# Three adapters around an attention and MLP block: laying x and the weights out feature-major and loading adapter 1's whole, on one core

## The reference

```python
def adapter(role, h0, W_down, b_down, W_up, b_up, gamma, beta):   # blocks 0, 2, 3
    h = gelu(h0 @ W_down[role] + b_down[role])                    # 256 -> 128
    y = h0 + h @ W_up[role] + b_up[role]                          # 128 -> 256
    return layernorm(y) * gamma[role] + beta[role]

def block1(x, target_codes):
    attn = softmax((x @ Wq) @ (x @ Wk).T / 16)                    # 32 x 32 for each sequence
    attn_out = attn @ (x @ Wv) @ Wp + bp
    cms_out = gelu(attn_out @ cW1 + cb1) @ cW2 + cb2 + one_hot(target_codes)
    modifier = gelu(concat(attn_out, cms_out) @ mW1 + mb1) @ mW2 + mb2
    return clip(x + cms_out + modifier, 0, 1)
```

## Time and profile before

| what | value |
|---|---|
| three runs | 195.41, 195.46, 195.92 us; median 195.46 |
| the profiled execution's own time | 195.86 us |
| its span, first to last instruction | 194.1 us |
| TensorE busy | 184.4 us, 95% of the span |
| VectorE busy | 114.2 us, 59% |
| ScalarE busy | 81.0 us, 42% |
| GpSimd busy | 42.2 us, 22% |
| DMA packets, bytes | 18,874 packets, 17.83 MB |

### The profile page before, as it was taken

The page is one execution under the profiler, slowest core; times in us unless marked ns, Lnnn a source line. Parts: engine busy times, 40 slices in busy tenths (PEclk is TensorE's granted clock), DMA queues, the critical chain, the costliest instruction groups (busy, mean ns, idle before and its releaser), DMA issues.

```text
span 194.1 us, 3155 instructions
## 1 busy us (share of the span) xinstructions
PE 184.4 (95%) x1031; PEld 158.1 (81%) x1031; DVE 114.2 (59%) x283; ACT 81.0 (42%) x164; POOL 42.2 (22%) x72
## 2 busy tenths in 40 slices
PE   7979999989999999999999999999999999999980
PEld 7858887979988888778888888888888989999860
DVE  2897998899658707983193532041432136558983
ACT  0643764544698306672055444003445323222340
POOL 8375657100000006000150000000100012226431
PEclk9999999999999999999999999999999999999997
DMA  3778579994301230330000061000100003441122
GB/s 105 233 206 285 156 254 286 261 295 159 108 3 17 93 108 0 108 111 0 0 0 3 0 181 35 0 0 5 54 0 0 3 0 106 120 130 68 41 60 77
DMA packets 18874, 17.83 MB, mean 92 GB/s; under 512 B 2145, under 2 KB 17322, under 8 KB 18858
## 3 DMA queue, kind: packets, MB, share of 16 engines
q1 hardware_dynamic: 17008, 14.79, 25.1%
q0 software_dynamic: 928, 2.11, 3.9%
q10 hardware_dynamic: 922, 0.73, 1.3%
HBM read 16.58 MB, written 1.05 MB: 91 GB/s over the span
## 4 chain that ended last, share of the span: by engine, by line
PE 78%; DVE 11%; DMA 4%; issue 2%; ACT 1%; POOL 1%; ACTq 0%; DVEq 0%
PE bank L639 20%; PE bank L641 19%; PE bank L640 19%; PE bank L751 5%; PE bank L767 5%; DMA stage<-in_L_cond_Wq 2%; PE bank L744 2%; DMA x_tok<-in_x,from_row_i 2%; PE bank L818 2%; PE bank L807 2%; PE bank L777 1%; DVE mw_l L1253 1%; DVE yA L1326 1%; PE bank L746 1%; DVE yB L1345 1%
## 5 line engine op out<-in xcount | busy, mean ns | idle before, releaser
L1407 DVE TENSOR_TENSOR g_l<-g_full,g_h 128x512 fp32r<-128x512 f32 x32 | 21.8, 690 | 36.1 <-ACT g_h L1033 36.0
L1030 ACT ACTIVATE g_full<-bank,vecs 128x512 f32<-128x512 f32 x32 | 22.1, 691 | 43.5 <-PE bank L641 40.5
L1519 POOL TENSOR_TENSOR mvA<-mvA,power 128x1 f32<-128x1 f32 x16 | 9.4, 590 | 70.4 <-DVE mvA L1262 70.4
L1033 ACT ACTIVATE g_h<-bank,vecs 128x512 fp32r<-128x512 f32 x32 | 22.0, 687 | 0.0
L1546 POOL TENSOR_TENSOR x1T<-x1T,cms_full 128x512 f32<-128x512 f32 x4 | 6.0, 1499 | 57.4 <-DVE cms_full L1422 57.3
L639 PE MATMUL bank<-g_h,mw_h 128*128 128x256 f32 (+1 forms) x48 | 16.0, 334 | 0.0
L641 PE MATMUL bank<-g_h,mw_l 128*128 128x256 f32 (+1 forms) x48 | 15.3, 318 | 0.0
L640 PE MATMUL bank<-g_l,mw_h 128*128 128x256 f32 (+1 forms) x48 | 15.3, 318 | 0.0
L639 PE MATMUL bank<-ao_h,mw_h 128*128 128x512 f32 x32 | 13.1, 411 | 0.0
L639 PE MATMUL bank<-ao_h,cw_h 128*128 128x512 f32 x32 | 12.8, 399 | 0.2
L641 PE MATMUL bank<-ao_h,mw_l 128*128 128x512 f32 x32 | 12.5, 391 | 0.0
(11 more groups left out here) (265 smaller groups left out, 442.5 us busy)
## 6 DMA issues: line engine op xcount, KB each, us to landing
stage<-in_L_cond_mW SPq DMA_DIRECT2D x6, 512.0 KB, 3.4
stage<-in_L_cond_cW SPq DMA_DIRECT2D x4, 512.0 KB, 6.0
wdA<-in_L_cond_W_down SPq DMA_DIRECT2D x14, 128.0 KB, 3.3
wuA<-in_L_cond_W_up SPq DMA_DIRECT2D x14, 128.0 KB, 3.6
wdB<-in_L_cond_W_down SPq DMA_DIRECT2D x12, 128.0 KB, 3.1
wuB<-in_L_cond_W_up SPq DMA_DIRECT2D x12, 128.0 KB, 3.0
wd_last<-in_L_cond_W_down SPq DMA_DIRECT2D x4, 128.0 KB, 2.4
wu_last<-in_L_cond_W_up SPq DMA_DIRECT2D x4, 128.0 KB, 2.6
```

The source lines that it names most:

```text
L1030: act.activation(g_full[n % 2][:, 0:width], bank[b][:, 0:width], ACT.Gelu, bias=bias)
L1033: act.activation(g[0][:, j, 0:width], bank[b][:, 0:width], ACT.Gelu, bias=bias).then_inc(g_high, 1)
L1407: dve.tensor_tensor(g[1][:, j, 0:width], g_full[n % 2][:, 0:width], g[0][:, j, 0:width].bitcast(F32), ALU.subtract).then_inc(g_ready, 1)
L1519: pool.tensor_tensor(mv[:, k, 2:3], mv[:, k, 1:2], power[:, :], ALU.pow).then_inc(done, 1)
```

## The change

The host lays the inputs out anew (`packed`): x feature by token, Wq, Wk and Wv transposed, W_down and W_up of a role side by side, all small vectors in one array as rows and in one as columns. The gathers of x, its transposes and copies (`load` on PE and ACT), the transposes of the squares and the transposition of the vectors (`vectors`) go. x (1 MB) and adapter 1's weights of all three roles (768 KB) each come in one DMA. POOL waits for the table of row numbers, loads them into registers (12, 12 and 8 at a time) and assembles each tile with four copies of 128 x (2 x 32); ACT copies the weights of the first four tiles out of `w_all`. Weights of the other tiles come by one DMA of 256 KB in place of two of 128 KB. `late_biases` and `first_bias` move from DVE to POOL as `biases`. `hot` of a full tile is no longer written out: the bias product reads a column of `hot_col` with stride 0. The row number of each token for the output and the mixed tiles' token roles are made in a new step `rows` during the MLP. `fold, 1` moves behind the first tiles, `codes` behind the second `split`, `mix` works in two pairs of tiles, and SP issues `piece(0)` after the weights of tile 4. The DVE sort now ends in `full_window` and `sorts` instead of `rows_of`; `sort_codes`, `seat2` and `rest_values` go.

The first entries of the plan, and the parts that the text speaks of:

```diff
-        ("warm", 10), ("fold_transpose", 0), ("fold_transpose", 1), ("warm", 3), ("order",), ("pick_vecs",),
-        ("fold_transpose", 2), ("spread",), ("fold", 0, 0), ("first_hot",), ("fold", 0, 1), ("fold_low", 0),
-        ("fold", 1, 0), ("chunk_vecs",), ("vectors",), ("sort_rest",), ("load", 0, 0), ("fold", 1, 1),
-        ("load", 0, 1), ("fold_low", 1), ("down", 0, 0), ("down", 0, 1), ("load", 0, 2), ("sort_codes",),
-        ("up", 0, 0), ("up", 0, 1), ("center", 0, 0), ("load", 0, 3), ("rest",), ("down", 0, 2), ("load", 0, 6),
-        ("down", 0, 3), ("center", 0, 1), ("up", 0, 2), ("late_biases",), ("turn", 0, 0), ("center", 0, 2),
-        ("up", 0, 3), ("load", 0, 7), ("seq_vecs",), ("turn", 0, 1), ("weights", 0, 0), ("center", 0, 3),
-        ("load", 0, 4), ("down", 0, 6), ("down", 0, 7), ("turn", 0, 2), ("up", 0, 6), ("up", 0, 7), ("turn", 0, 3),
-        ("center", 0, 6), ("split", 0, 0), ("load", 0, 5), ("down", 0, 4), ("center", 0, 7), ("token_tables",),
+        ("warm", 18), ("biases", 0), ("fold", 0, 0), ("fold", 0, 1), ("order",), ("load", 0, 0), ("first_weights", 0),
+        ("pick_vecs",), ("first_hot",), ("warm", 4), ("chunk_vecs",), ("load", 0, 1), ("first_weights", 1), ("warm", 6),
+        ("fold_low", 0), ("load", 0, 2), ("down", 0, 0), ("first_weights", 2), ("down", 0, 1), ("load", 0, 3),
+        ("sort_rest",), ("first_weights", 3), ("fold", 1, 0), ("up", 0, 0), ("spread",), ("up", 0, 1), ("center", 0, 0),
+        ("rest",), ("down", 0, 2), ("load", 0, 6), ("down", 0, 3), ("center", 0, 1), ("up", 0, 2), ("fold", 1, 1),
+        ("turn", 0, 0), ("center", 0, 2), ("up", 0, 3), ("load", 0, 7), ("seq_vecs",), ("turn", 0, 1),
+        ("weights", 0, 0), ("center", 0, 3), ("load", 0, 4), ("down", 0, 6), ("down", 0, 7), ("turn", 0, 2),
+        ("up", 0, 6), ("up", 0, 7), ("turn", 0, 3), ("fold_low", 1), ("center", 0, 6), ("split", 0, 0), ("load", 0, 5),
+        ("down", 0, 4), ("center", 0, 7),
         ("turn", 0, 6), ("down", 0, 5), ("project", 0, 0), ("weights", 0, 1), ("turn", 0, 7), ("up", 0, 4),
-        ("project", 0, 1), ("split", 1, 0), ("center", 0, 4), ("up", 0, 5), ("codes",), ("turn", 0, 4),
-        ("center", 0, 5), ("scores", 0), ("values", 0, 0), ("probs", 0), ("values", 0, 1), ("turn", 0, 5),
-        ("split", 1, 1), ("weights", 1), ("mix", 0), ("weights", 2), ("project", 1, 0), ("project", 1, 1),
+        ("project", 0, 1), ("split", 1, 0), ("center", 0, 4), ("up", 0, 5), ("turn", 0, 4),
+        ("center", 0, 5), ("biases", 1), ("scores", 0), ("values", 0, 0), ("probs", 0), ("values", 0, 1), ("turn", 0, 5),
+        ("split", 1, 1), ("codes",), ("weights", 1), ("mix", 0), ("weights", 2), ("project", 1, 0), ("project", 1, 1),
         ("values", 1, 0), ("scores", 1), ("probs", 1), ("values", 1, 1), ("hidden", 0, 0), ("hidden", 0, 1),
-        ("hidden", 0, 2), ("hidden", 0, 3), ("hidden", 0, 4), ("weights", 3), ("mix", 1), ("hidden", 0, 5),
+        ("hidden", 0, 2), ("hidden", 0, 3), ("rows",), ("token_tables",), ("hidden", 0, 4), ("weights", 3), ("mix", 1), ("hidden", 0, 5),
...
+            sp.dma_start(ids[:, :], a["ids"]).then_inc(ids_in, 16)
+            sp.wait_ge(bu_zero, 1)
+            sp.dma_start(bu_rows[0:2 * R, :, :], a["b_up"]).then_inc(bu_in, 16)
+            sp.dma_start(x_all[:, :, :], a["x"]).then_inc(x_all_in, 16)
+            sp.dma_start(w_all[:, :, :], a["adapters"][0].rearrange("r p n -> p r n")).then_inc(w_all_in, 16)
+            for w in "vp":
+                sp.dma_start(wT[w][:, :, :], square_from(w)).then_inc(square_in[w], 16)
...
 
-                if p == 1:
-                    sp.wait_ge(wT_ps, 2)
-                elif p == 2:
-                    sp.wait_ge(fold_ps, KD)
-                elif p > 2:
+                if p > 2:
                     sp.wait_ge(w_ready, p - STAGE + 1)
                 sp.dma_start(view(slot), src).then_inc(stage_in[slot], 16)
...
-            def fetch(layer, r, down, up, down_in, up_in):
-                sp.dma_start(down[:, :, :],
-                             a[down_w[layer]].rearrange("r (k p) n -> r p k n", p=P)[bass.ds(r, 1), :, :, :]
-                             .rearrange("r p k n -> (r p) k n")).then_inc(down_in, 16)
-                sp.dma_start(up[:, :],
-                             a[up_w[layer]][bass.ds(r, 1), :, :].rearrange("r p n -> (r p) n")).then_inc(up_in, 16)
+            def fetch(layer, r, w, w_in):
+                sp.dma_start(w[:, :], a["adapters"][(0, 2, 3).index(layer)][bass.ds(r, 1), :, :]
+                             .rearrange("r p n -> (r p) n")).then_inc(w_in, 16)
...
             sp.wait_ge(chunks_ready, 1)
             load_roles(range(FULL))
-            for n in range(PASSES):
+            for n in range(COPIED, PASSES):
+                if n == 2 * WSLOTS:
+                    piece(0)
                 if passes_of(0)[n] == (MESSY[0], FULL):
                     sp.wait_ge(rest_roles_ready, 1)
...
                 pe.wait_ge(sorts_ready, 1)
-                take(1, rows_in_ready, 1)
-                pe.matmul(bank[1][:, 0:FULL], seat[:, :], rows_of[:, :], start=True, stop=True).then_inc(order_ps, 1)
+                pe.wait_ge(constants, 2)
+                take(2, seats_ready, 1)
+                pe.matmul(bank[2][:, 0:FULL * WB], row_spread[:, :], sorts[:, 0:FULL * WB],
+                          start=True, stop=True).then_inc(order_ps, 1)
...
-                pe.wait_ge(code_sorts_ready, 1)
-                take(6, codes_ready, 1)
-                pe.matmul(bank[6][:, 0:B], spread[:, 1, :], sorts[:, :], start=True, stop=True).then_inc(codes_ps, 1)
-
...
-                left, right = (("q", "k"), ("v", None))[n]
+                left, right = ("qk", "vp")[n]
                 if m == 0:
                     take(2 * n + 1, fold_ready, n + 1)
-                    pe.wait_ge(wT_ready, 2 + n)
-                    if n:
-                        pe.wait_ge(square_in["p"], 16)
+                    pe.wait_ge(square_in[left], 16)
+                    pe.wait_ge(square_in[right], 16)
                 for t in range(KD):
...
-                    pe.wait_ge(xA_ready, i + 1)
-                    x, done = xA[i % XSLOTS], downA_ps
+                    if layer == 0:
+                        pe.wait_ge(x0_ready, i + 1)
+                        x, done = x0[i], downA_ps
...
+                if c in MESSY:
+                    hot = hot_mixed[:, c - MESSY[0], :]
+                else:
+                    hot = hot_col[:, full_column(c):full_column(c) + 1].to_broadcast([P, P])
...
+                for q in range(2):
+                    pe.wait_ge(values_ready, 2 * h + q + 1)
+                    for m in range(KD):
+                        for n in (2 * q, 2 * q + 1):
+                            mm = pe.matmul(bank[m][:, n * P:(n + 1) * P], values_tok[h][:, n, m * P:(m + 1) * P],
+                                           probs_T[:, n, :], start=True, stop=True)
+                        if q:
+                            mm.then_inc(mix_ps, 1)
...
+            for w in "qk":
+                act.dma_start(wT[w][:, :, :], square_from(w)).then_inc(square_in[w], 16)
+            act.dma_start(vec_rows[:, :], a["vec_rows"][0:PER_ROLE * R, :]).then_inc(vectors_in, 16)
+            act.dma_start(vecs[:, :], a["vecs"]).then_inc(vecs_in, 16)
...
+            def first_weights(n):
+
+                if n == 0:
+                    act.wait_ge(chunks_ready, 1)
+                    _, values = nc.values_load_multi_w_load_instructions(
+                        chunk_role_i[0:1, 0:COPIED], engines=[mybir.EngineType.Activation], min_val=0, max_val=R - 1,
+                        skip_runtime_bounds_check_because="VectorE makes these numbers of two comparisons")
+                    first_role.extend(values)
+                    act.wait_ge(w_all_in, 16)
+                act.copy(wA[n][:, :], w_all[:, bass.ds(first_role[n], 1), :].rearrange("p r n -> p (r n)")).then_inc(wA_in[n], 16)
...
+                dve.memset(bu_rows[:, :, :], 0.0).then_inc(bu_zero, 1)
...
-                dve.tensor_scalar(from_row_i[:, 0:FULL], bank[1][:, 0:FULL], tok_col[:, 0:1], None,
-                                  ALU.add).then_inc(rows_in_ready, 1)
+                dve.tensor_copy(seat_row_i[:, 0:FULL, :].rearrange("p w j -> p (w j)"),
+                                bank[2][:, 0:FULL * WB]).then_inc(seats_ready, 1)
...
+            def rows_of_tokens():
+
+                for j in range(WB):
+                    part = slice(S * j, S * (j + 1))
+                    dve.tensor_copy(token_role_i[part, :], rest_role[part, :].rearrange("p (w j) -> p w j", j=WB)[:, :, j])
+                    ins = dve.tensor_scalar(from_row_i[part, :], seat_row_i[part, :, j], tok_col[part, 0:1], None, ALU.add)
+                ins.then_inc(rows_in_ready, 1)
...
+                for lo, first, n in ((0, 0, MESSY[0]), (MESSY[0], FULL, 2), (MESSY[1] + 1, MESSY[0], 2)):
```

(55 more changed lines are left out.)

345 lines of the change are left out of this document (119 added, 226 removed).

## The result

The changed kernel takes 199.24 us (median of four runs: 197.55, 198.72, 199.75, 199.83) against 195.69: ratio 1.0154, 95% interval 1.0107 to 1.0201, so it is slower. The forecast of 195.7, with a range up to 198.0, was too low. Its profiled execution took 199.83 us with a span of 198.0, 3.9 us more than before.

A forecast was written before the change was run, and what follows sets the result against it. PE bounds the kernel from 50 us on, so only an earlier first hidden pays. Terms -2.4 + 2.6 - 0.33 + 0.3 = +0.2 us gave 196.1 profiled, 195.7 median, no change; own range 195.0 to 197.0, wider 193.5 to 198.0.

The forecast's parts named there:

- (b): Before the first down: PE reaches the sorting product behind warming products and fold, at 9.7 us; row numbers at 10.35.
- (c): Before the first down: POOL loads 12 row numbers into registers in 1.35 us, until 11.7.
- (d): Before the first down: POOL's four copies take 0.7 us a tile, bounds 0.3 and 1.3; first tile at 12.4.
- its landing: Before the first split: piece(0), issued 7.75 us behind the first down, lands between 11.2 and 13.75, taken as 11.6.
- biases beside the probabilities: Between scores and mix: POOL's biases 1 arithmetic slows DVE's probability chain by 0.3 us, range 0 to 1.0.
- `mix` in pairs: Behind the split: brings nothing, since mix waits for the probabilities and not for the second half of the values.
- `rows` on DVE: During the MLP: eight small instructions cost nothing, as DVE is idle between hidden steps; 1.4 us without that cover.
- rival D: Before the first split: piece(0) takes 6.0 us, landing at 13.75 instead of 11.6; total 197.8 us, chance 0.05.
- head start: The first down starts at 12.4 instead of 14.83 us, 2.4 us earlier.
- (a): Before the first down: the sort, with one instruction more (0.3 us), ends by 7.8 us.
- rival B: Start: clock rises at 4.5 instead of 6.7, 1.1 us less; a tile costs 0.3, 0.4 less; 194.2 us, chance 0.35.
- rival C: Before the split: POOL becomes the bound if a tile costs 1.3 us, deciding from 0.84 on; 197.7 us, chance 0.20.

The follow-up runs named there:

- e12: Changed kernel with piece(0), tile 5 and tile 7 early, biases 1 later, sorting product first, and mix in its old order: 194.49 us, ratio 0.9931.
- e2: Changed kernel with tile 5's POOL copies ahead of the inverse deviations of tiles 6 and 7: 197.12 us, ratio 1.0078 to the kernel before.
- e1: Changed kernel with piece(0) issued early, ahead of SP's wait for the roles of the mixed tiles: 197.82 us, ratio 1.0099 to the kernel before.
- e5: Kernel before with piece(0) issued late, behind tile 4's weights as in the changed kernel: 200.37 us, ratio 1.0241.
- e11: Changed kernel with warming products added where PE stands idle, 12 behind up(0,7) and 5 ahead of down(0,5): 199.29 us, ratio 1.0180 to the kernel before.
- e8: Changed kernel with SP issuing nothing behind piece(0) until that has landed: 197.44 us, ratio 1.0082 to the kernel before.
- e6: Changed kernel with piece(0) issued early and POOL's copies of tile 5 and tile 7 moved early: 194.76 us, ratio 0.9941 to the kernel before.
- e14: Changed kernel with six warming products ahead of the first down taken out: 198.38 us, ratio 1.0123 to the kernel before.
- e3: Changed kernel with both piece(0) issued early and tile 5's POOL copies moved early: 195.56 us, ratio 0.9995 to the kernel before.

## Why the prediction was wrong

Counted by its own steps:

| step | forecast | measured |
|---|---|---|
| (b) sorting product, row numbers | 9.7, 10.35 | 9.60, 10.2 |
| (c) POOL starts to copy | 11.7 | 11.48 |
| (d) one tile by POOL | 0.7 (0.3 to 1.3) | 0.74 |
| first `down` | 12.4 | 12.82 (11.72 to 12.97 in other profiles of the same start) |
| issue of `piece(0)` behind the first `down` | 7.75 | 7.28 |
| DVE asks for it | 9.65 | 9.16 |
| its landing | 3.8 | **6.0** |
| DVE's stall | 2.0 | **4.17** |
| PE idle ahead of `down` 7 | 2 | 0.67 |
| first `down` to end of split | 17.45 | 18.93 |
| `down` 5, ahead of `project` | not costed | **+1.26** |
| `codes` moved | -0.33 | -0.20 |
| biases beside the probabilities | +0.3 (0 to 1.0) | +0.37 |
| `mix` in pairs | 0 | 0 (e12) |
| `rows` on DVE | 0 | 0.28 of the 0.36 behind the first `hidden` |

**The step that failed first** is the size of one term: "A transfer of this size lands after 3.4 us (mW) or, with a full queue, 6.0 (cW) ... With some 0.4 us of the 512 KB ahead of it still to move I take 11.6." The place, the wait and both ends of the bound were right; the value was taken from the low end, the mW pieces, which go out with little else under way, while this one goes out among 3.3 MB issued within five microseconds. It landed after 6.0 us instead of 3.8: that is +2.2 us, of which 0.5 came back because it was issued earlier than forecast and 0.2 because the instructions behind it were shorter. The line came out at 18.93 us instead of 17.45. That was rival D, given 5 in 100. Its split (+2.3 against before) is the +2.07 measured. The row to go by was the cW row: three of its four members are issued behind the adapter weights, between 24.80 and 31.9 us, and landed after 5.4, 9.0 and 6.6 us.

**The second failure** is an omission. Tile 5's copies come from the same POOL queue as tile 7's, and I followed that queue only as far as tile 7. Behind `split, 0, 0` in the plan stands `load, 0, 5`: in the kernel before that was a gather that nobody waited for, now it is 0.74 us of copies which can start only after the inverse deviation of tile 7, in the very 1.96 us of DVE's split. The four copies have durations of 236 to 1316 ns there, and DVE's two instructions keep their 0.69 and 1.23 us. I had the earlier trace rows for this contention and used it for the biases only. The Trainium skill (SBUF — State Buffer, section "SBUF: two separate sides") gives the reason as a lock held for a whole instruction; the longest copy, 1316 ns beside one of 1.23 us, agrees with it. With tile 5 ahead of the split (e2) both parts of this wait vanish.

**Third, the clock.** That idle time of PE can have the lower clock behind it was in none of the cases. It lengthened three profiled runs (e1, e5, the changed kernel again); its share of the median is not shown (e11).

**The head start** came out at 2.0 instead of 2.4 for a reason that none of steps (a) to (d) names: I took PE to wait for POOL's first tile, and PE was still busy with ten warming products of its own. They start only when the 36 before them are done. In the profiled run these ended at 7.95 us, just as forecast, but in other profiles of the same plan they took from 5.79 us (e8) to 7.04 (e6):

```profile
1.05 5.79 PE L619 MATMUL bank<-warm 128*128 128x128 f32 x36 [1.05 <-DVE warm L1016]
...
1.05 7.04 PE L618 MATMUL bank<-warm 128*128 128x128 f32 x36 [1.05 <-DVE warm L1015]
```

The number of these records that start in one microsecond went from 7 to 11, between 4 and 6 us in e8 and only at 7 us in e6. So rival B's mechanism (the rise moves) is real: from the earliest to the latest it moves the start by 1.25 us. The Trainium skill's statement on that moment (TensorE: Matmul & The Clock Gate, "What's actually happening"), that it moves between runs, is shown by these; one trace could not show it. It was no rival to the stall, though: with the clock early and `piece(0)` late the kernel is still slower than before (e2, e8, e14).

**What held**: the sort doesn't decide; a tile is 0.74 us, so rival C (from 0.84 on) did not come about; `hot` with stride 0 costs nothing (its weight load takes 190 ns like the others); `codes`, `mix` and the biases within 0.15 us of their terms. Behind the first `hidden` 0.36 us were added where the forecast had nothing. PE's idle time ahead of `down` 7 was short because the products before it came 0.7 us later than I had them; the line through POOL was there, 2.3 us shorter than the stage's (e1), and it bound as soon as the stage no longer did (e3, e6).

## What to carry to other kernels

A DMA that is moved behind others is priced by the transfers issued around its new place, those behind it too, and not by the median that its shape has elsewhere. When work moves to another engine's in-order queue, follow that queue to its last entry and ask for each entry what it stands behind and which long DVE instruction runs beside it. An early start is worth what the first late thing behind it leaves: here two reordered entries and one moved DMA turned a loss of 1.5 to 1.8% into a gain of 0.6%; with later biases, the sorting product first and fewer fill products it was 1.25%.

## What the runs showed of the hardware

- TensorE's granted clock fell to 0.50 behind idle times of 1.5 to 3.7 us in three profiles (e1, e5, the changed kernel again) and stayed at 1.00 behind idle times of 1.1 to 2.4 us in four others (the changed kernel, e2, e8, e14). In the changed kernel the way to the first `hidden` was 1.8 us longer in the profile where it fell; the eight runs of e1 lie in two groups of four, 1.9 us apart, with mean granted clocks of 0.993 and 0.982.
- Under an unbroken row of warming products from 1.05 us on, the products speeded up at different moments: 36 records took 5.79 to 7.04 us. The granted clock is shown as 1.00 on both sides of that moment.
- A 512 KB transfer that lands after 3.2 to 3.8 us when little else is under way (the mW pieces issued between 44 and 75 us) took 4.8 us behind 512 KB (e8), and 5.1 to 6.3 us in five profiles with more behind it as well.
- POOL's copy of 64 numbers a partition takes 0.18 us in a row of them (2.95 us for 16) and up to 1.3 us beside a DVE subtraction of 1.23 us.
